# Causal 16-head attention: four banks for the maxima, two for the exponentials, one reduction for two heads

## Chip, core and metric

One core of one Trainium2 chip runs the whole program. The metric is the device time of the program in microseconds (us). The engines named below are TensorE (PE, its weight loads PEld), VectorE (DVE), ScalarE (ACT), GpSimd (POOL) and SyncE (SP, which issues DMAs). PSUM is the memory that TensorE writes its products to; it has eight banks of 512 f32 per partition.

## What is computed

The reference is eight layers on x of shape (16, 512, 128), each of the form x = x + f(layernorm(x)): causal attention with 16 heads (layer 0), a mixture of experts, window attention, the mixture again, rotary attention with 16 heads (layer 4), a channel mix, a gated delta rule, and the channel mix again. The change touches the function that builds layers 0 and 4, and by its flag `causal` only layer 0 is built differently. Layer 0 computes, per batch element:

```python
H = 16; D = C // H                       # 16 heads of 8 channels
qkv = x @ w_qkv + b_qkv                  # x: (16, 512, 128) after layernorm
scores = einsum('bhqd,bhkd->bhqk', q, k) / sqrt(D)
scores = where(tril, scores, -inf)
attn = softmax(scores)                   # over 512 keys
out = einsum('bhqk,bhkd->bhqd', attn, v)
return out @ w_out + b_out
```

## The kernel before

`attention16` works in a software pipeline over the 16 batch elements ("sequences" in the code). In the body for one index, TensorE computes the row maxima of the next element (the maxima pass) and the exponentials and their product with V for the present element (the exponential pass), besides projections, transposes and the output product of neighbours. The order of each engine's instructions is written out by hand, slot by slot.

**Slots.** A body has 32 slots `u`, in four quads of eight (`PER_QUAD`); a quad is four heads, a slot is two heads (`g` = 0 and 1) of one query tile of 128. In the causal layer a slot of the maxima pass covers W = 128 * (t + 1) keys, t = u % 8 // 2, so 128 columns in slots 0 and 1 of a quad, 256 in 2 and 3, 384 in 4 and 5, and 512 in 6 and 7 (L244). The exponential pass goes the other way: 512 columns in slots 0 and 1, 384, 256, and 128 in 6 and 7 (L245, Q0).

**TensorE's order in a slot** (L562 to L583): whatever the shared PSUM bank `misc` is used for at this slot (most even slots have one use); then for head 0 and then head 1: the scores for the maximum into `max_bank` (`max_product`, L494), the scores for the exponential into `exp_bank` (`exp_product`, L516), and two small products that add the causal mask to the former (`max_mask`, L500, the second of which tells DVE). After each odd slot of a quad follow eight products with V (`pv`, L479): after slot 1 the 128-column ones of the quad before, after slot 3 the 512-column ones (which first wait for ACT to have copied `out_bank` away, L602), after slot 5 those of 384, after slot 7 those of 256.

**Rings.** `max_bank` and `exp_bank` have three banks each (`RING`); head number h uses bank h % 3. Before a product into the maxima ring TensorE waits for the reduction of head h - 3 (`max_free`, L488); before one into the exponential ring it waits for ACT's exponential of head h - 3 (`exp_free`, L511). `out_bank` and `misc` take the other two banks.

**DVE** (L681 to L704) reduces each head's bank to one column of `M` (L687), and in some slots evacuates `misc`: in slots 14, 18, 24 and 30 it normalises four heads (L673, L676), in slot 22 it adds the output to x (L700). **ACT** (L639 to L655) does the exponential of each head (L646), in slot 2 of each quad the copy of `out_bank` (L602), and the copies out of `misc` for the transposed input (slot 0, L609), Q and K (slots 4 and 8, L617), the transposed output (slot 16, L636), V (slot 26, L624) and the maxima (slots 2, 12, 20, 28, L634). **POOL** masks the diagonal of the exponentials (L397).

A use of `misc` waits for its last evacuation, on whichever engine that is.

Of the kernel before, what the change touches and what calls it, by code (L numbers as in the profile page):

```python
# [8 lines left out]
AX = mybir.AxisListType  # L9

P = 128
B, T, C = 16, 512, 128
# [129 lines left out]
QUADS = H // 4  # L142
SLOTS = TPS * PAIRS
PER_QUAD = SLOTS // QUADS
PARTS = 3
RING = 3

Q_SLOTS = [(0, 3, 0), (3, 2, 1), (5, 1, 2)]
K_SLOTS = [(0, 3), (3, 2), (5, 1)]
# [29 lines left out]
def wait_positive(eng, sem, value):  # L179

    if not isinstance(value, int) or value > 0:
        eng.wait_ge(sem, value)


def attention16(nc, tag, io, X, stats, identity, causal, rope, biased):
    with Stage(nc, tag) as s:
# [27 lines left out]
        on = s.sb("on", [P, TPS, C])  # L214
        oT = s.sb("oT", [P, T])
        parts_dram = s.dram("parts_dram", (2, 2, PARTS, P, T), BF16)
        max_bank = s.ps("max_bank", [P, RING, T])
        exp_bank = s.ps("exp_bank", [P, RING, T])
        out_bank = s.ps("out_bank", [P, T])
        misc = s.ps("misc", [P, T])  # L220

# [36 lines left out]
        def max_head(b, u, g):  # L258

            return 2 * SLOTS * (b.off + 1) + 2 * u + g  # L260

        def exp_head(b, u, n):

            return 2 * SLOTS * b.off + 2 * u + n

        def misc_uses(b):

# [189 lines left out]
        def _(pe):  # L457
# [26 lines left out]
            def max_free(b, u, g):  # L484
                to = (b.par + 1) % 2
                if g == 0 and u % (SLOTS // 2) == 0:
                    pe.wait_ge(qk_in[to][u // (SLOTS // 2)], loads_before(b, to))
                wait_positive(pe, max_done, max_head(b, u, g) - RING + 1)  # L488

            def max_product(b, u, g):  # L490

                to = (b.par + 1) % 2
                j, t, i = u // PER_QUAD, u % PER_QUAD // 2, 2 * (u // PER_QUAD) + u % 2
                return nc.tensor.matmul(max_bank[:, max_head(b, u, g) % RING, 0:W[t]], QS[64 * g:64 * g + ROWS, to, i, t * P:(t + 1) * P],  # L494
                                        KS[64 * g:64 * g + ROWS, to, i, 0:W[t]], start=True, stop=True)

            def max_mask(b, u, g, c):

                rows, at = slice(64 * g, 64 * g + 64), (u % PER_QUAD // 2) * P + 64 * c
                return nc.tensor.matmul(max_bank[:, max_head(b, u, g) % RING, at:at + 64], mask64[rows, c, :], ident64[rows, :],  # L500
                                        start=False, stop=True, skip_group_check=True)

            def loads_before(b, to):
# [4 lines left out]
            def exp_free(b, u, n):  # L508
                if n == 0 and u % PER_QUAD == 0:
                    pe.wait_ge(shift_in[u // PER_QUAD], b.at(32, 32))  # L510
                wait_positive(pe, exp_done, exp_head(b, u, n) - RING + 1)  # L511

            def exp_product(b, u, n):
                g = EXP_ORDER[n]
                kb, i = u % PER_QUAD // 2, 2 * (u // PER_QUAD) + u % 2
                return nc.tensor.matmul(exp_bank[:, exp_head(b, u, n) % RING, Q0[kb]:T],  # L516
                                        KS[64 * g:64 * g + ROWS + 1, b.par, i, kb * P:(kb + 1) * P],
                                        QS[64 * g:64 * g + ROWS + 1, b.par, i, Q0[kb]:T],
                                        start=True, stop=True)

            def body(pe, b):
                to = (b.par + 1) % 2
                uses_at = {}
                for n, (u, what) in enumerate(misc_uses(b)):
                    uses_at.setdefault(u, []).append((what, misc_base(b) + n))

                def misc_use(what, index):
                    wait_positive(pe, misc_free, index)
                    kind = what[0]
                    if kind == "HT":  # L530
                        pe.wait_ge(hn_ready, b.at(1, 3))
                        for t in range(TPS):
                            last = nc.tensor.transpose(misc[:, t * P:(t + 1) * P], hn[:, t, :], identity[:, :])
                    elif kind in ("Q", "K", "QS", "KS"):
                        name = {"Q": "q", "K": "k", "QS": "q_swapped", "KS": "k_swapped"}[kind]
                        last = nc.tensor.matmul(misc[:, :], w[name][:, :], hT[:, b.par, :], start=True, stop=True)
                    elif kind == "V":
                        for t in range(TPS):
                            last = nc.tensor.matmul(misc[:, t * P:(t + 1) * P], hT[:, to, t * P:(t + 1) * P],
                                                    w["v"][:, :], start=True, stop=True)  # L540
                    elif kind == "MAX":
                        j = what[1]
                        seq = 0 if j == 3 else 1

                        pe.wait_ge(max_done, b.at(2 * SLOTS, (seq * QUADS + j + 1) * 2 * PER_QUAD))
                        last = nc.tensor.transpose(misc[0:H, 0:P], M[:, j % 2, :], identity[:, :])
                    elif kind == "HEADS":
                        j = what[1]
                        pe.wait_ge(heads_kept, b.at(QUADS, j + 1 - (QUADS if j == 3 else 0)))
                        for t in range(TPS):  # L550
                            last = nc.tensor.transpose(misc[:, t * P:(t + 1) * P],
                                                       heads_out[:, j % 2, t * P:(t + 1) * P], identity[:, :])
                    elif kind == "OT":
                        for t in range(TPS):
                            last = nc.tensor.transpose(misc[:, t * P:(t + 1) * P], on[:, t, :], identity[:, :])
                    else:
                        for t in range(TPS):
                            last = nc.tensor.matmul(misc[:, t * P:(t + 1) * P], oT[:, t * P:(t + 1) * P],
                                                    w["out"][:, :], start=True, stop=True)
                    last.then_inc(misc_full, 1)  # L560

                for u in range(SLOTS):  # L562
                    for what, index in uses_at.get(u, []):
                        misc_use(what, index)
                    for n in range(2):
                        if b.maxes:
                            max_free(b, u, n)
                            last = max_product(b, u, n)
                            if not causal:
                                last.then_inc(max_scores, 1)  # L570
                        if b.exp:
                            exp_free(b, u, n)
                            exp_product(b, u, n).then_inc(scores, 1)
                        if b.maxes and causal:
                            max_mask(b, u, n, 0)
                            max_mask(b, u, n, 1).then_inc(max_scores, 1)
                    for j in range(QUADS):
                        for v in range(NV):
                            slot = PER_QUAD * j + PVS[v][3]
                            if slot == u and b.exp:  # L580
                                pv(b, 0, j, v)
                            if slot == u + SLOTS and b.finish:
                                pv(b, -1, j, v)  # L583
# [4 lines left out]
        def _(act):  # L588
# [49 lines left out]
            def body(act, b):  # L638
                for u in range(SLOTS):  # L639
                    if b.exp:  # L640
                        j, n, kb = u // PER_QUAD, u % PER_QUAD, u % PER_QUAD // 2
                        wait_positive(act, pv_done, b.at(QUADS * NV, (j - 1) * NV + LAST_OF[kb]))
                        for h in range(2):
                            e = exp_head(b, u, h)
                            act.wait_ge(scores, e + 1)
                            nc.scalar.activation(probs[:, n, EXP_ORDER[h], Q0[kb]:T], exp_bank[:, e % RING, Q0[kb]:T],  # L646
                                                 ACT.Exp, scale=float(D) ** -0.5).then_inc(exp_done, 1)
                    for j in range(QUADS):
                        if u == PER_QUAD * j + KEEP_AT and b.exp:
# [10 lines left out]
        def _(dve):  # L660
# [19 lines left out]
            def body(dve, b):  # L680
                for u in range(SLOTS):  # L681
                    if b.maxes:
                        j, t = u // PER_QUAD, u % PER_QUAD // 2
                        for g in range(2):
                            col = 8 * g + 4 * (u % 2) + t
                            dve.wait_ge(max_scores, b.at(2 * SLOTS, 2 * SLOTS + 2 * u + g + 1))
                            nc.vector.reduce_max(M[:, j % 2, col:col + 1],  # L687
                                                 max_bank[:, max_head(b, u, g) % RING, 0:W[t]], AX.X)\
                                .then_inc(max_done, 1)
                    for n, (slot, what) in enumerate(misc_uses(b)):  # L690
                        if slot != u or what[0] not in ("HEADS", "Y"):
# [2402 lines left out]
```

## Time and profile before

| | us |
|---|---|
| median of 3 runs | 5264.1 |
| lowest, highest | 5263.89, 5328.75 |
| the profiled execution | 5352.55 |
| its span, first to last instruction | 5350.5 |
| causal layer within it, first product to last (62:1011) | 949 |

The profile is of one execution. Busy times are of an engine's own work and overlap between engines; a matmul's end is modelled, so a busy TensorE is not one at its peak. "PEclk" is the TensorE clock that was granted, as a share of 2.4 GHz: 1.00 is 2.4 GHz, 0.50 is 1.2 GHz, and a value between is a mean over a stretch that holds both. In a timeline row "x4" means four instructions merged into one row, and the bracket says how long the engine was idle before and what ended that.

### The profile page before, as it was taken

How to read it: one execution, taken by the hardware profiler on the slowest of the kernel's cores; microseconds unless marked ns; L12 is line 12 of the kernel's file. 1: busy time of each engine (PE TensorE's matmuls, PEld its weight loads, DVE VectorE, ACT ScalarE, POOL GpSimd, SP SyncE). 2: the span in 40 equal slices, each digit the busy share in tenths (PEclk: the TensorE clock that was granted, in tenths of full speed). 3: DMA queues.
4: the chain of work that ended last, by engine and by line, in shares of the span. 5: the costliest groups of instructions: out<-in, count | busy, mean ns of one | idle time of the engine just before them, and what ended most of it. 6: DMA issues, size and time to landing. Idle time of an engine off the chain costs nothing. (4 is left out here: it accounts for less than half of the span.)

```text
span 5350.5 us, 180273 instructions
## 1 busy us (share of the span) xinstructions
PE 4132.0 (77%) x73116; PEld 2507.2 (47%) x73118; DVE 3108.1 (58%) x7520; ACT 2378.0 (44%) x5497; POOL 1808.8 (34%) x2620
## 2 busy tenths in 40 slices
PE   4999989629359999999376399999957799996555
PEld 2443444319325555555265033333335688884223
DVE  5555555334446666665334488888676555514887
ACT  1544454305235555554043077777835433313443
POOL 3333333140455555553312422323112233302442
PEclk9776676659679999999588599999977799997777
DMA  2111111211100000000111111111001211162001
GB/s 72 46 42 40 46 40 40 64 38 52 51 11 2 3 2 2 2 2 2 50 52 52 47 45 50 49 48 49 25 2 63 84 39 45 22 194 77 24 24 33
DMA packets 252950, 218.39 MB, mean 41 GB/s; under 512 B 63683, under 2 KB 221316, under 8 KB 252550
## 3 DMA queue, kind: packets, MB, share of 16 engines
q1 hardware_dynamic: 244358, 196.20, 12.0%
q0 software_dynamic: 8192, 16.79, 1.1%
q8 instruction: 259, 4.24, 0.3%
q14 instruction: 141, 1.16, 0.1%
HBM read 139.24 MB, written 73.14 MB: 40 GB/s over the span
## 5 line engine op out<-in xcount | busy, mean ns | idle before, releaser
L687 DVE TENSOR_REDUCE l_M<-l_max_bank 128x1 f32<-128x512 f32 (+3 forms) x2048 | 1083.1, 583 | 583.6 <-PE l_max_bank L500 417.8
L646 ACT ACTIVATE l_probs<-l_exp_bank 128x512 f32<-128x512 f32 (+3 forms) x2048 | 950.0, 523 | 637.5 <-PE l_exp_bank L516 632.6
L494 PE MATMUL l_max_bank<-l_KS,l_QS 48*128 48x512 bf16 (+3 forms) x2048 | 650.5, 391 | 105.7 <-DVE l_M L687 51.2
L479 PE MATMUL l_out_bank<-l_probs,l_V 128*32 128x256 f32 (+2 forms) x6144 | 587.5, 466 | 71.3 <-ACT l_heads_out L602 71.2
L516 PE MATMUL l_exp_bank<-l_QS,l_KS 49*128 49x512 bf16 (+3 forms) x2048 | 625.3, 378 | 18.4 <-ACT l_probs L646 13.4
L397 POOL TENSOR_SCALAR_AFFINE_SELECT l_probs<-l_probs 128x256 f32<-128x256 f32 x512 | 208.0, 406 | 603.7 <-ACT l_probs L646 601.3
L494 PEld LDWEIGHTS l_max_bank<-l_KS,l_QS 48*128 48x128 bf16 x2048 | 162.0, 98 | 469.7 <-DVE l_M L687 235.8
L1841 DVE TENSOR_REDUCE l_M<-l_max_bank 128x4 f32<-128x512 f32 x256 | 175.5, 686 | 172.6 <-PE l_max_bank L1655 172.6
L479 PEld LDWEIGHTS l_out_bank<-l_probs,l_V 128*32 128x32 f32 x6144 | 137.8, 114 | 283.7 <-ACT l_probs L646 131.2
L871 POOL DMA_INDIRECT l_back<-main_sorted_out,l_index x128 | 122.5, 957 | 413.5 <-issue 413.2
L500 PE MATMUL l_max_bank<-l_ident,l_mask 64*128 64x64 bf16 x2048 | 246.1, 218 | 0.0
L1496 POOL TENSOR_TENSOR l_rms<-l_rms,l_minus_half 128x20 f32<-128x20 f32 x64 | 226.1, 3532 | 11.8 <-POOL l_rms L1493 11.8
L500 PEld LDWEIGHTS l_max_bank<-l_ident,l_mask 64*128 64x128 bf16 x2048 | 197.7, 115 | 63.9 <-issue 39.3
L436 POOL TENSOR_TENSOR l_qk<-l_qk,l_cos 128x512 f32<-128x512 f32 x32 | 40.7, 1270 | 526.6 <-ACT l_rot L620 526.4
L516 PEld LDWEIGHTS l_exp_bank<-l_QS,l_KS 49*128 49x128 bf16 x2048 | 177.9, 98 | 80.3 <-ACT l_probs L646 68.1
L969 ACT ACTIVATE l_hidden<-l_up_bank,l_own 128x128 f32<-128x128 f32 x584 | 166.4, 368 | 86.7 <-PE l_up_bank L919 86.7
L1721 ACT ACTIVATE l_raw<-l_misc 128x512 f32<-128x512 f32 (+1 forms) x192 | 101.5, 529 | 222.4 <-PE l_misc L1558 221.1
L915 PE MATMUL l_t_bank<-main_identity,l_rows 128*128 128x128 f32 x148 | 49.5, 334 | 186.0 <-DMA l_rows<-main_sorted_in 185.8
L857 POOL DMA_INDIRECT main_sorted_in<-l_hn,l_index x128 | 124.8, 975 | 189.6 <-DVE l_hn L1000 151.2
L1633 PE MATMUL l_out_bank<-l_V,l_probs 64*64 64x65 f32 x2048 | 175.8, 227 | 1.3 <-issue 1.3
L1641 PE MATMUL l_out_bank<-l_V,l_probs 64*64 64x65 f32 x2048 | 175.9, 227 | 0.0
L1635 PE MATMUL l_out_bank<-l_V,l_probs 64*64 64x65 f32 x2048 | 175.8, 227 | 0.0
(419 smaller groups left out, 10323.2 us busy)
## 6 DMA issues: line engine op xcount, KB each, us to landing
l_parts_dram<-l_parts SPq DMA_DIRECT2D x64, 384.0 KB, 2.6
l_fir_band<-in_dr_short_dram SPq DMA_DIRECT2D x16, 1024.0 KB, 6.2
l_fir_band<-in_dr_long_dram SPq DMA_DIRECT2D x16, 1024.0 KB, 8.5
l_QS<-l_parts_dram SPq DMA_DIRECT2D x128, 96.0 KB
l_KS<-l_parts_dram SPq DMA_DIRECT2D x128, 96.0 KB
l_kqv_dram<-l_in_out SPq DMA_DIRECT2D x16, 768.0 KB, 3.6
l_core_ring<-l_kqv_dram SPq DMA_DIRECT2D x48, 256.0 KB, 3.2
l_rows<-main_sorted_in SPq DMA_DIRECT2D x152, 64.0 KB, 1.8
```

The costliest lines, as they stand in the source:

```text
L397: nc.gpsimd.affine_select(out=diagonal, in_=diagonal, compare_op=ALU.is_ge, fill=0.0, base=0, pattern=[[0, 2], [1, P]], channel_multiplier ...
L479: last = nc.tensor.matmul(out_bank[STRIP * h:STRIP * (h + 1), q0:q1], V[:, par, kb, 4 * j + h, :], probs[:, 2 * kb + h // 2, h % 2, q0:q1] ...
L494: return nc.tensor.matmul(max_bank[:, max_head(b, u, g) % RING, 0:W[t]], QS[64 * g:64 * g + ROWS, to, i, t * P:(t + 1) * P], KS[64 * g:64 ...
L500: return nc.tensor.matmul(max_bank[:, max_head(b, u, g) % RING, at:at + 64], mask64[rows, c, :], ident64[rows, :], start=False, stop=True, ...
L516: return nc.tensor.matmul(exp_bank[:, exp_head(b, u, n) % RING, Q0[kb]:T], KS[64 * g:64 * g + ROWS + 1, b.par, i, kb * P:(kb + 1) * P], QS ...
L646: nc.scalar.activation(probs[:, n, EXP_ORDER[h], Q0[kb]:T], exp_bank[:, e % RING, Q0[kb]:T], ACT.Exp, scale=float(D) ** -0.5).then_inc(exp ...
L687: nc.vector.reduce_max(M[:, j % 2, col:col + 1], max_bank[:, max_head(b, u, g) % RING, 0:W[t]], AX.X)\
L1496: g.tensor_tensor(rms[:, :], rms[:, :], minus_half[:, :], ALU.pow).then_inc(rms_ready, 1)
L1633: nc.tensor.matmul(o[top], now[top, top], v, start=begin_a or (t == 0 and a == 0), stop=True, skip_group_check=True)
L1635: last = nc.tensor.matmul(o[low], now[top, low], v, start=begin_a, stop=True, skip_group_check=True)
L1641: last = nc.tensor.matmul(o[low], now[low, top], V[low, par, t, j, :], start=begin_a, stop=True, skip_group_check=True)
L1841: v.reduce_max(M[:, t % 2, h:h + REP], max_bank[:, r, :].rearrange("p (a k) -> p a k", a=REP), AX.X).then_inc(max_done, 1)
```

## The change

The three-bank rings stay for the rotary layer. In the causal layer `max_bank` gets four banks and `exp_bank` two. One reduction on DVE now reads both heads of a slot (two neighbouring banks, W columns of each) and writes two columns of `M`, eight apart. It waits until both heads' scores are masked. The semaphore `max_done` counts one per slot in place of one per head, `maxima_of` converts, and TensorE waits for it once per slot, before head 0: for the reduction of the slot two before. The exponential of head h - 2 must be done before the product of head h.

```diff
-RING = 3
+RINGS = {True: (4, 2), False: (3, 3)}
...
-        max_bank = s.ps("max_bank", [P, RING, T])
-        exp_bank = s.ps("exp_bank", [P, RING, T])
+        MAX_RING, EXP_RING = RINGS[causal]
+        max_bank = s.ps("max_bank", [P, MAX_RING, T])
+        exp_bank = s.ps("exp_bank", [P, EXP_RING, T])
...
+        def maxima_of(heads):
+
+            return (heads + 1) // 2 if causal else heads
...
-                wait_positive(pe, max_done, max_head(b, u, g) - RING + 1)
+                if g == 0 or not causal:
+                    wait_positive(pe, max_done, maxima_of(max_head(b, u, g) - MAX_RING + 1))
...
-                wait_positive(pe, exp_done, exp_head(b, u, n) - RING + 1)
+                wait_positive(pe, exp_done, exp_head(b, u, n) - EXP_RING + 1)
...
-                        pe.wait_ge(max_done, b.at(2 * SLOTS, (seq * QUADS + j + 1) * 2 * PER_QUAD))
+                        pe.wait_ge(max_done, maxima_of(b.at(2 * SLOTS, (seq * QUADS + j + 1) * 2 * PER_QUAD)))
...
-                        for g in range(2):
-                            col = 8 * g + 4 * (u % 2) + t
-                            dve.wait_ge(max_scores, b.at(2 * SLOTS, 2 * SLOTS + 2 * u + g + 1))
-                            nc.vector.reduce_max(M[:, j % 2, col:col + 1],
-                                                 max_bank[:, max_head(b, u, g) % RING, 0:W[t]], AX.X)\
+                        m, col = max_head(b, u, 0), 4 * (u % 2) + t
+                        if causal:
+                            dve.wait_ge(max_scores, m + 2)
+                            nc.vector.reduce_max(M[:, j % 2, col:col + 9:8],
+                                                 max_bank[:, m % MAX_RING:m % MAX_RING + 2, 0:W[t]], AX.X)\
+                                .then_inc(max_done, 1)
+                        for g in range(0 if causal else 2):
+                            dve.wait_ge(max_scores, m + g + 1)
+                            nc.vector.reduce_max(M[:, j % 2, col + 8 * g:col + 8 * g + 1],
+                                                 max_bank[:, (m + g) % MAX_RING, 0:W[t]], AX.X)\
                                 .then_inc(max_done, 1)
```

The other lines replace `RING` by `MAX_RING` or `EXP_RING` in the bank indices of L494, L500, L516 and L646.

## Rows read from the trace of the kernel before

**Rows 1.** The page: span, and busy time of each engine.
```profile
span 5350.5 us, 180273 instructions
PE 4132.0 (77%) x73116; PEld 2507.2 (47%) x73118; DVE 3108.1 (58%) x7520; ACT 2378.0 (44%) x5497; POOL 1808.8 (34%) x2620
```

**Rows 2.** Windows; columns: each engine's busy us, then PEclk, DMA share, GB/s.
```profile
62.00:109.00 47.00, 33.10 (x222) 18.31 (x223) 27.85 (x69) 4.19 (x8) 7.04 (x8) 1.00 0.22 71
109.00:984.00 875.00, 790.02 (x6531) 352.58 (x6526) 464.35 (x1146) 436.62 (x1184) 311.91 (x621) 0.72 0.13 40
```

**Rows 3.** Windows: the four quads of one batch element in the steady state.
```profile
564.72:581.61 16.89, 15.81 (x108) 5.67 (x105) 7.12 (x18) 7.39 (x21) 5.19 (x11) 0.60 0.15 47
581.61:597.01 15.40, 14.09 (x109) 5.87 (x104) 7.56 (x19) 7.09 (x19) 8.19 (x14) 0.60 0.15 52
597.01:611.07 14.06, 12.96 (x117) 6.55 (x112) 8.88 (x24) 6.99 (x20) 3.25 (x8) 0.71 0.18 57
611.07:622.76 11.69, 9.82 (x115) 5.44 (x113) 7.61 (x22) 6.94 (x19) 4.23 (x9) 1.00 0.02 5
```

**Rows 4.** Waits of PE, PEld in 109:984: us in total, times, longest us.
```profile
PE l_out_bank L479 <- ACT l_heads_out L602: 32.7, 61, 0.6
PE l_max_bank L494 <- DVE l_M L687: 23.0, 65, 0.5
...
PEld l_max_bank L494 <- DVE l_M L687: 85.4, 232, 1.2
PEld l_exp_bank L516 <- ACT l_probs L646: 48.3, 141, 1.4
```

**Rows 5.** DVE groups by form (first two 109:984): busy us, mean ns, idle before.
```profile
L687 DVE TENSOR_REDUCE l_M<-l_max_bank 128x1 f32<-128x512 f32 x240 | 152.6, 683 | 87.0 <-PE l_max_bank L500 87.0
...
L687 DVE TENSOR_REDUCE l_M<-l_max_bank 128x1 f32<-128x128 f32 x240 | 60.9, 286 | 64.3 <-PE l_max_bank L500 62.1
...
L1841 DVE TENSOR_REDUCE l_M<-l_max_bank 128x4 f32<-128x512 f32 x256 | 175.5, 686 | 172.6 <-PE l_max_bank L1655 172.6
```

**Rows 6.** Timeline, last slots of a quad, clock full; start, us, work, idle before.
```profile
561.82 1.29 DVE L687 TENSOR_REDUCE l_M<-l_max_bank 128x1 f32<-128x512 f32 x2 [0.84 <-PE l_max_bank L500]
563.30 0.29 DVE L676 TENSOR_TENSOR l_on<-l_misc,l_rec 128x128 f32<-128x128 f32 x1
...
562.57 0.39 PE L494 MATMUL l_max_bank<-l_KS,l_QS 48*128 48x512 bf16 x1 [0.45 <-DVE l_M L687]
563.65 0.66 PE L533 MATMUL l_misc<-main_identity,l_hn 128*128 128x128 f32 x4
```

**Rows 7.** Timeline, first four slots of a quad, clock full.
```profile
553.03 2.07 ACT L646 ACTIVATE l_probs<-l_exp_bank 128x512 f32<-128x512 f32 x4 [1.56 <-PE l_exp_bank L516]
...
556.64 0.60 ACT L602 ACTIVATE l_heads_out<-l_out_bank 128x512 f32<-128x512 f32 x1
...
553.69 0.39 PE L516 MATMUL l_exp_bank<-l_QS,l_KS 49*128 49x512 bf16 x1
...
557.39 1.06 PE L479 MATMUL l_out_bank<-l_probs,l_V 128*32 128x512 f32 x8 [0.63 <-ACT l_heads_out L602]
```

**Rows 8.** Timeline, the same slots with the clock at half.
```profile
592.85 1.29 DVE L687 TENSOR_REDUCE l_M<-l_max_bank 128x1 f32<-128x512 f32 x2 [2.44 <-PE l_max_bank L500]
...
593.60 0.61 PE L494 MATMUL l_max_bank<-l_KS,l_QS 48*128 48x512 bf16 x1
...
595.26 1.12 PE L555 MATMUL l_misc<-main_identity,l_on 128*128 128x128 f32 x4
...
597.66 0.61 PE L516 MATMUL l_exp_bank<-l_QS,l_KS 49*128 49x512 bf16 x1
...
597.01 1.08 ACT L646 ACTIVATE l_probs<-l_exp_bank 128x512 f32<-128x512 f32 x2 [2.48 <-PE l_exp_bank L516]
```

**Rows 9.** Timeline of ACT: a copy between the exponentials of slots 0 and 1.
```profile
507.67 0.61 ACT L609 ACTIVATE l_hT<-l_misc 128x512 f32<-128x512 f32 x1
508.14 1.88 ACT L646 ACTIVATE l_probs<-l_exp_bank 128x512 f32<-128x512 f32 x4
```

More of the change, by code:

```diff
@@ L493, in max_product @@
                 j, t, i = u // PER_QUAD, u % PER_QUAD // 2, 2 * (u // PER_QUAD) + u % 2
-                return nc.tensor.matmul(max_bank[:, max_head(b, u, g) % RING, 0:W[t]], QS[64 * g:64 * g + ROWS, to, i, t * P:(t + 1) * P],
+                return nc.tensor.matmul(max_bank[:, max_head(b, u, g) % MAX_RING, 0:W[t]], QS[64 * g:64 * g + ROWS, to, i, t * P:(t + 1) * P],
                                         KS[64 * g:64 * g + ROWS, to, i, 0:W[t]], start=True, stop=True)
@@ L499, in max_mask @@
                 rows, at = slice(64 * g, 64 * g + 64), (u % PER_QUAD // 2) * P + 64 * c
-                return nc.tensor.matmul(max_bank[:, max_head(b, u, g) % RING, at:at + 64], mask64[rows, c, :], ident64[rows, :],
+                return nc.tensor.matmul(max_bank[:, max_head(b, u, g) % MAX_RING, at:at + 64], mask64[rows, c, :], ident64[rows, :],
                                         start=False, stop=True, skip_group_check=True)
@@ L515, in exp_product @@
                 kb, i = u % PER_QUAD // 2, 2 * (u // PER_QUAD) + u % 2
-                return nc.tensor.matmul(exp_bank[:, exp_head(b, u, n) % RING, Q0[kb]:T],
+                return nc.tensor.matmul(exp_bank[:, exp_head(b, u, n) % EXP_RING, Q0[kb]:T],
                                         KS[64 * g:64 * g + ROWS + 1, b.par, i, kb * P:(kb + 1) * P],
@@ L645, in body @@
                             act.wait_ge(scores, e + 1)
-                            nc.scalar.activation(probs[:, n, EXP_ORDER[h], Q0[kb]:T], exp_bank[:, e % RING, Q0[kb]:T],
+                            nc.scalar.activation(probs[:, n, EXP_ORDER[h], Q0[kb]:T], exp_bank[:, e % EXP_RING, Q0[kb]:T],
                                                  ACT.Exp, scale=float(D) ** -0.5).then_inc(exp_done, 1)
```

## The prediction, made before the changed kernel had run

> **What bounds the kernel now.** The page first: a span of 5350.5 us with TensorE busy for 4132.0 of it, DVE for 3108.1 [rows 1]. Only the causal layer is built differently, so I cut the trace there. Its maxima pass runs alone for 47 us, then maxima and exponentials run together for 875 us [rows 2]: fifteen sequences of 58.04 us each (16.89 + 15.40 + 14.06 + 11.69 [rows 3], quads 0 to 3), 16% of the span. In those 875 us TensorE is busy for 790, DVE for 464, ACT for 437 [rows 2]. Neither DVE nor ACT is near full; TensorE is, but its clock is only granted at 0.72 on the mean. The quads show what that means: the one at 1.00 takes 11.69 us, those at 0.60 take 15.40 and 16.89 [rows 3]. A clock of 0.60 is a fifth of the time at full and the rest at half. So in quad 1 some 3.1 us at full do 3.1/11.69 = 0.26 of it and 12.3 us at half the remaining 0.74, or 16.7 us a quad at half. By the same step quad 0 is 19 and quad 2 16.3; quad 3 I take as 17. A sequence all at full would be 4 x 11.69 = 46.8 us, one all at half 69.
>
> Next the waits that the rings make. TensorE proper idles 23.0 us on the reductions and its weight loads 85.4 [rows 4]; the first is time in which nothing was running, the second includes time in which earlier matmuls were still at work, so a gain from the maxima ring lies between 23 and 85 us over the layer. Waits for ACT to leave a bank of the exponential ring show as 48.3 in the weight loads [rows 4]. The largest wait of TensorE proper, 32.7 us in 61 times, is none of these: it is the product with V that waits for ACT's copy of out_bank [rows 4], once in every quad.
>
> **One reduction for two.** The mean is 286 ns for 128 elements and 683 for 512 [rows 5], so 1.034 ns an element and 154 ns on top. A pair at 512 costs 154 + 1024 x 1.034 = 1.21 us, at 128 0.42. Two single ones back to back take 1.29 us from start to end [rows 6], not 1.37, because they overlap: the change takes only 0.08 us per slot off DVE, 41 us over 512 slots, on an engine that is half idle. More outputs in one reduction cost nothing: four columns out of 512 elements take 686 ns [rows 5].
>
> The Trainium skill (Perfetto Trace Analysis, Optimizing Scalar/DVE Operations) says that grouping helps where the engine is saturated, and that where it isn't but makes bubbles on others, breaking instructions up may finish work sooner. By it this step is the wrong way round; by the rows it is even, as follows.
>
> The pair starts when the second head is ready, not the first. At the end of a quad with full clock the first reduction starts at 561.82 and both are done at 563.11 [rows 6]. The second head's scores follow the first's by 0.03 us or so there (its mask product is issued right after), so the pair runs from 561.87 to 563.08: the same end. That end matters, for DVE then normalises until 563.59, and TensorE's next transposes start at 563.65 [rows 6], just behind it. **So at full clock the stall of 0.45 us before the fourth maximum product [rows 6] goes, and the wait for the normalisation takes its place: nothing gained** there.
>
> At half clock the fourth maximum product starts at 593.60, behind the first reduction as before, but the product itself takes 0.61 us, not 0.39, so TensorE comes there 0.2 later and the stall is 0.25. The transposes at 595.26 come long after DVE's first reductions are done (594.14), with a normalisation of half a microsecond behind them [rows 8]: here the 0.25 is gained. In the sequence of [rows 3] the ends of quads 0 and 1 fall at half clock, those of 2 and 3 at full: 0.25 + 0.25, and I allow 0.1 in quad 2. Gain: 0.6 us per sequence.
>
> **Two exponential banks.** In slots 0 and 1 of a quad the exponentials are 512 wide: four take 2.07 us [rows 7], so one takes 0.60 and they follow each other every 0.49. With three banks only the fourth product waits, for the first exponential: it ends at 553.63 and the product starts at 553.69 [rows 7]. With two banks the third product starts there and the fourth waits for the second exponential, which ends at 554.12: 554.18, 0.49 us later. At half clock it is the same: 597.66 is 0.05 behind the end of the first exponential of 597.01 [rows 8]; the new fourth start is 598.15. Queued behind that product are its two mask products, the products with V of the last quad, the use of misc, and slots 2 and 3. Does it reach the end? ACT itself loses nothing: the fourth product lands before ACT is through the third. Where ACT has a copy between slots 0 and 1 it is what is late: the copy at 507.67 puts the next exponentials at 508.14 and they run back to back until 510.02 into slot 2 [rows 9]. That is so in quads 0, 1 and 2 (copies of the transposed input, K, the transposed output); there I take 0.2 us, the extra latency from bank free to product to exponential, except where half clock makes TensorE the late one, in quad 2 (0.5). Quad 3 has no such copy: 0.5. Sum 0.2 + 0.2 + 0.5 + 0.5 = 1.4 us.
>
> In slots 2 and 3 the third and fourth products wait 0.4 to 0.6 us more than now, but the product with V behind them starts at 557.39, after ACT's copy (556.64 + 0.60) [rows 7], which hangs on slot 2's exponentials alone: nothing. In slots 4 and 5 the wait for the second exponential of 0.38 us lands within 0.05 of where the wait for the first reduction was: 0.2 per sequence. If the cover by ACT's copies is thinner than I think, quads 0 and 1 cost 0.5 each too: 2.0 + 0.2.
>
> **Edges.** The maxima pass alone (47 us, DVE busy 27.85 [rows 2]) saves 0.08 us in each of 32 slots, up to 2.5 us; the last sequence, with exponentials alone, loses 0.5 us in four quads: 2. Even. The DMA queue waits on the same events as before and no POOL or SP step is moved.
>
> **Sum.** 15 x (1.4 + 0.2 - 0.6) = 15 us more. Against the profiled execution, 5352.55 us with 2.05 outside its span, that is 5368; this execution is 88 us above the median, and the three runs lie between 5263.89 and 5328.75, so I carry the difference to the median: 5264.1 + 15 = **5279 us**. Bounds: all of the 85.4 us gained and nothing lost is 5179; 0.5 us lost in each of 60 quads and none gained, 5297.
>
> **The rivals.**
> *The clock falls more often.* The clock is at full for the whole of quad 3 and falls a fifth of the way into quad 0 [rows 3], just after its slots 0 and 1. The change thins TensorE's work in exactly these slots, by 0.2 to 0.5 us. If quad 3 too goes to half, it takes 17 us in place of 11.69: 5.3 us, 80 over fifteen, 5264 + 80 = 5344. If all of a sequence is at half: 15 x 11 = 165, 5429. It decides as soon as quad 3 no longer holds 1.00. For it: the clock sits at the edge, since it falls in every sequence. Against: slots 6 and 7 get denser. The Trainium skill (TensorE: Matmul & The Clock Gate, A second HAM failure mode) describes PSUM cycling whose micro-idles make the clock oscillate; quads at 0.60 and 1.00 in turn agree with it.
> *The maxima ring pays in full.* The weight loads' 85.4 us are the price, and the exponential ring's is hidden: 5264 - 85 + 5 = 5184. Against it: the transposes that sit 0.06 us behind the normalisation. With it the clock may hold: if quads 1 and 2 stay at full, 15 x (15.40 + 14.06 - 23.38) = 91 us more, 5093. It decides where TensorE stops waiting in slots 4 to 7.
> *The reduction does not join.* If DVE takes two banks in one instruction at the price of two separate starts (1.37 us), the normalisation ends 0.16 later at full clock, in two quads: 15 x 0.3 = 5 more, 5284.
>
> **Chances.** The sum as forecast, or either bound of its waits, 0.60; DVE not joining 0.05; maxima ring in full 0.12, with the clock 0.07 beside it; one more fall per sequence 0.12, all at half 0.04. A measurement of this kernel tells a change from none at about 2%, 105 us. Beyond it below lies the 0.07, above the 0.04 and part of the 0.12: slower 0.09, same 0.84. The range: 5184 and 5344 are the ends of the next cases; the runs before differ by 65 us by themselves, so I go to 5190 and 5350.
>
> **What will show it.** Right: paired reductions near 1.21 us; the weight loads' wait of L494 for DVE under 20 us; the wait of L516 for ACT over 100 us; the wait for the normalisation before L533 in its place; the full-clock quad at 12.0 to 12.2 us, and the sequence near 59. Wrong: a quad at full clock under 11.5 us, or a mean clock of the 875 us that leaves 0.72 by over 0.05 either way, which would outweigh every term above.

## The result, and the profile after

Twenty runs of the changed kernel have a median of 5279.23 us (5269.66 to 5291.3). The kernel before, run twenty times beside it, has 5326.89 (5260.22 to 5345.13). The ratio is **0.9938, 95% interval 0.9913 to 0.9964**: 0.6% faster, where I had forecast 15 us slower. The ratio is of means and leaves out the three runs of the kernel before that lie more than 1.5% above its fastest; by the medians the gain is 47.7 us. That the forecast's figure of 5279 agrees with the median is luck: it was built on 5264.1, the median of three runs of which two lay in the lower of two groups. Of the twenty runs four lie between 5260 and 5280 and sixteen between 5306 and 5345. The changed kernel has no such spread.

The page of the changed kernel, to set beside [rows 1]:

```profile
span 5281.6 us, 179763 instructions
PE 4062.9 (77%) x73118; PEld 2451.1 (46%) x73118; DVE 3078.2 (58%) x7008; ACT 2388.1 (45%) x5497; POOL 1812.4 (34%) x2620
```

The span is 68.9 us shorter; the profiled execution of the kernel before, 5352.55 us, lies above all twenty of its runs, so this is more than the 47.7 of the medians. The last exponential of the causal layer starts at 949.2 us, where it was at 1010.1, so 61 of the 68.9 are in this layer. Its windows (each engine's busy us, then PEclk, DMA share, GB/s): first the stretch with both passes, which answers to the second of [rows 2], then the four quads of one batch element (a "sequence", from the first exponential of its quad 0 to that of the next), then a quad 0, a quad 2 and a whole sequence.

```profile
103.00:938.00 835.00, 747.98 (x6625) 313.04 (x6625) 441.67 (x674) 452.15 (x1204) 317.72 (x631) 0.82 0.13 42
...
420.35:437.05 16.70, 16.13 (x104) 5.14 (x102) 6.52 (x8) 7.68 (x20) 4.95 (x10) 0.59 0.14 45
437.05:452.25 15.20, 14.30 (x108) 5.69 (x105) 6.97 (x10) 7.27 (x20) 8.22 (x14) 0.60 0.13 45
452.25:466.77 14.52, 13.19 (x117) 5.99 (x112) 8.57 (x15) 7.03 (x19) 3.35 (x8) 0.71 0.23 64
466.77:478.98 12.21, 10.39 (x115) 5.05 (x113) 7.40 (x13) 7.14 (x20) 4.50 (x9) 1.00 0.02 5
...
478.98:490.65 11.67, 10.62 (x104) 3.95 (x102) 6.48 (x8) 7.51 (x20) 4.75 (x10) 1.00 0.22 66
555.58:567.89 12.31, 10.42 (x115) 5.06 (x113) 8.57 (x16) 7.03 (x19) 3.27 (x8) 1.00 0.28 85
212.71:263.48 50.77, 44.99 (x434) 19.30 (x432) 29.29 (x46) 28.82 (x77) 20.94 (x41) 0.90 0.15 49
```

**The sequence at 420.35 has quads at 0.59, 0.60, 0.71 and 1.00, as the third to the fourteenth all had before** [rows 3], and there the two kernels can be compared at the same clock: 16.70 against 16.89, 15.20 against 15.40, 14.52 against 14.06, 12.21 against 11.69. The sum is 58.63 against 58.04: with the clock falling in the same quads, the change costs 0.6 us per sequence. But of the sequences of the changed kernel only two are like that. The others of the second to the thirteenth take 50.8 to 53.9 us, like the one at 212.71 with 0.90 of the clock and 50.77 us; ten of these twelve have a quad 0 at 1.00, before it was one. The mean clock of the stretch rises from 0.72 [rows 2] to 0.82. TensorE is busy for 747.98 us in it where it was for 790.02 [rows 2], though the change takes no product away: 42 us less of busy time in a stretch that is 40 us shorter.

The waits of PE and PEld in that stretch (us in total, times, longest us), to set beside [rows 4]:

```profile
PE l_exp_bank L522 <- ACT l_probs L652: 42.1, 110, 0.7
PE l_out_bank L484 <- ACT l_heads_out L608: 8.6, 35, 0.2
PE l_misc L557 <- DVE main_X L711: 7.8, 14, 0.6
PE l_misc L539 <- DVE l_on L682: 5.9, 13, 0.5
PE l_misc L561 <- DVE l_on L682: 4.3, 9, 0.6
PE l_max_bank L500 <- DVE l_M L693: 1.3, 2, 0.9
...
PEld l_exp_bank L522 <- ACT l_probs L652: 185.7, 460, 1.2
...
PEld l_max_bank L500 <- DVE l_M L693: 22.7, 66, 1.2
```

The kernel before, the waits of PE that [rows 4] leave out:

```profile
PE l_exp_bank L516 <- ACT l_probs L646: 8.6, 22, 0.5
PE l_misc L546 <- ACT l_hT L609: 3.4, 14, 0.4
PE l_misc L551 <- DVE main_X L700: 2.4, 14, 0.2
```

They moved as forecast. TensorE proper waited 23.0 us for the maxima ring and waits 1.3. For the exponential ring it waited 8.6 us and waits 42.1, and its weight loads 185.7 where they waited 48.3; the loads' wait for the maxima ring is 22.7, just above the "under 20" of the forecast. New in TensorE proper are the waits for DVE's normalisation before the transposes. The wait for ACT's copy of `out_bank` shrank from 32.7 us to 8.6, for part of the new wait falls ahead of it. In total TensorE proper waits 70 us in these stretches, before and after. **The 40 us come with the clock, then, not with the waits.**

Paired reductions by form (busy us, mean ns, idle before), to set beside [rows 5]: 1221 ns for twice 512 elements where 1212 was worked out, 426 for twice 128 where it was 418.

```profile
L693 DVE TENSOR_REDUCE l_M<-l_max_bank 128x2 f32<-128x1024 f32 x122 | 147.4, 1221 | 61.0 <-PE l_max_bank L506 61.0
...
L693 DVE TENSOR_REDUCE l_M<-l_max_bank 128x2 f32<-128x256 f32 x120 | 51.1, 426 | 65.3 <-PE l_max_bank L506 61.5
```

The start of a quad 3 at full clock (start, us, work, idle before), to set beside [rows 7]:

```profile
623.66 2.22 ACT L652 ACTIVATE l_probs<-l_exp_bank 128x512 f32<-128x512 f32 x4 [1.94 <-PE l_exp_bank L522]
...
624.31 0.39 PE L522 MATMUL l_exp_bank<-l_QS,l_KS 49*128 49x512 bf16 x1 [0.36 <-ACT l_probs L652]
624.80 0.39 PE L522 MATMUL l_exp_bank<-l_QS,l_KS 49*128 49x512 bf16 x1
625.12 0.43 PE L484 MATMUL l_out_bank<-l_probs,l_V 128*32 128x128 f32 x8
```

The third product starts 0.05 us after the first exponential's end and the fourth 0.49 later, at 624.80; before the change the fourth started where the third does now. The end of that quad, to set beside [rows 6]:

```profile
633.02 1.23 DVE L693 TENSOR_REDUCE l_M<-l_max_bank 128x2 f32<-128x1024 f32 x1 [0.85 <-PE l_max_bank L506]
...
634.45 0.29 DVE L682 TENSOR_TENSOR l_on<-l_misc,l_rec 128x128 f32<-128x128 f32 x1
...
634.79 0.66 PE L539 MATMUL l_misc<-main_identity,l_hn 128*128 128x128 f32 x4 [0.46 <-DVE l_on L682]
```

The stall of 0.45 us before the fourth maximum product is gone, and in its place TensorE waits 0.46 us for the normalisation (634.45 + 0.29), before the transposes. The end of a quad 0 has no normalisation. The kernel before had the same stall there at full clock, and the changed kernel has no wait of TensorE at that place:

```profile
172.59 0.39 PE L494 MATMUL l_max_bank<-l_KS,l_QS 48*128 48x512 bf16 x1 [0.45 <-DVE l_M L687]
```

### The profile page after: what moved, and what is told of

Same layout as the page of the kernel before. It is cut to its first block and busy times, and to the rows that moved or that the text cites. A ratio compares the mean times of both kernels' runs of the same rounds, so it can differ in the third digit from the quotient of the medians.

```text
span 5281.6 us, 179763 instructions
## 1 busy us (share of the span) xinstructions
PE 4062.9 (77%) x73118; PEld 2451.1 (46%) x73118; DVE 3078.2 (58%) x7008; ACT 2388.1 (45%) x5497; POOL 1812.4 (34%) x2620
## 5 line engine op out<-in xcount | busy, mean ns | idle before, releaser
L698 DVE TENSOR_REDUCE l_M<-l_max_bank 128x1 f32<-128x512 f32 x1024 | 635.2, 681 | 157.6 <-PE l_max_bank L500 157.3
L500 PE MATMUL l_max_bank<-l_KS,l_QS 48*128 48x512 bf16 (+3 forms) x2048 | 620.6, 376 | 80.6 <-DMA l_KS<-l_parts_dram 45.2
L693 DVE TENSOR_REDUCE l_M<-l_max_bank 128x2 f32<-128x256 f32 (+3 forms) x512 | 416.1, 824 | 386.7 <-PE l_max_bank L506 382.0
L484 PE MATMUL l_out_bank<-l_probs,l_V 128*32 128x256 f32 (+2 forms) x6144 | 558.0, 444 | 48.2 <-ACT l_heads_out L608 45.8
L500 PEld LDWEIGHTS l_max_bank<-l_KS,l_QS 48*128 48x128 bf16 x2048 | 159.8, 97 | 393.4 <-DVE l_M L698 147.1
L1507 POOL TENSOR_TENSOR l_rms<-l_rms,l_minus_half 128x20 f32<-128x20 f32 x64 | 226.2, 3534 | 11.8 <-POOL l_rms L1504 11.6
L506 PE MATMUL l_max_bank<-l_ident,l_mask 64*128 64x64 bf16 x2048 | 229.2, 208 | 0.0
```

The source lines that it names most:

```text
L484: last = nc.tensor.matmul(out_bank[STRIP * h:STRIP * (h + 1), q0:q1], V[:, par, kb, 4 * j + h, :], probs[:, 2 * kb + h // 2, h % 2, q0:q1] ...
L500: return nc.tensor.matmul(max_bank[:, max_head(b, u, g) % MAX_RING, 0:W[t]], QS[64 * g:64 * g + ROWS, to, i, t * P:(t + 1) * P], KS[64 * g ...
L506: return nc.tensor.matmul(max_bank[:, max_head(b, u, g) % MAX_RING, at:at + 64], mask64[rows, c, :], ident64[rows, :], start=False, stop=T ...
L693: nc.vector.reduce_max(M[:, j % 2, col:col + 9:8], max_bank[:, m % MAX_RING:m % MAX_RING + 2, 0:W[t]], AX.X)\
L698: nc.vector.reduce_max(M[:, j % 2, col + 8 * g:col + 8 * g + 1], max_bank[:, (m + g) % MAX_RING, 0:W[t]], AX.X)\
L1507: g.tensor_tensor(rms[:, :], rms[:, :], minus_half[:, :], ALU.pow).then_inc(rms_ready, 1)
```

## The experiments

Two theories were set against each other. **Ring theory:** the change wins because TensorE waits less, by four banks or by the joined reduction. **Clock theory:** at equal clock the change loses a little; it wins since the kernel before falls into step with the granted clock, the same falls in each sequence, and any change to the length of a sequence breaks that step. In e2 to e8 layers 1 to 7 are left out (`build(nc, io, layers=(0,))`), so that only the causal layer counts; their times are compared with each other. e2 to e4 ran on one chip and e5 to e8 on another; the whole kernel before, run beside them, has medians of 5325.16 and 5336.91 us, 0.2% apart, where the differences that are read across the two groups are 2.7% and more.

**e1: the kernel before, unchanged.**

> The unchanged kernel once more, for a second trace of it and for the spread of its time. Clock theory: its 20 earlier runs lie in two groups, four from 5260 to 5280 us and sixteen from 5306 to 5345; a trace of the lower group must show the causal layer's sequences shorter than 58 us at a mean clock above 0.72 and the quads at clock 1.00 still at 11.7 us; one of the upper group must repeat the 58.04 us. Ring theory (the change wins by its waits): the groups have nothing to do with the causal layer, its sequences are 58 us in either.

Measured: 5330.99 us (5261.21 to 5339.96, 12 runs), ratio 0.9991 (0.9965 to 1.0017). One run of twelve, 5261.21 us, is in the lower group; its mean clock over the program is 0.857, that of the others 0.838 to 0.847. The traced one (5320.52 us) has the same 58.0 us from its fourth sequence to the thirteenth; the first row is such a sequence, the second a quad 0 of an early sequence that had the full clock:

```profile
320.96:378.96 58.00, 52.64 (x434) 23.54 (x432) 31.16 (x79) 28.42 (x77) 20.84 (x42) 0.71 0.13 43
155.32:167.21 11.89, 10.03 (x107) 4.26 (x105) 7.07 (x18) 7.28 (x20) 5.19 (x11) 1.00 0.21 67
```

So the step is no accident of one execution. No run of the lower group has a trace, so what its sequences look like is not shown.

**e2: layer 0 of the kernel before, alone.**

> The kernel before with layers 1 to 7 left out (load, layer norm, causal attention, store), for a time in which only the causal layer counts. From the trace of before: load and norm 62 us, layer 949, store some 10 to 20: 1025 to 1040 us if the clock falls twice per sequence as in that trace; 960 to 990 in runs where it does not. Clock theory: both values occur, or a value between them. Ring theory: one value near 1030.

Measured: 1018.14 us (1006.96 to 1027.11). Three of the six runs lie at 1006.96 to 1011.68 and three at 1024.60 to 1027.11: two values, as clock theory had it, but neither of them near its 960 to 990, and the upper near the 1030 of ring theory. The times alone don't decide. The trace (1006.96 us, clock 0.778) says more: six sequences of 46 to 58 us first, then the step sets in with the seventh, and each takes 57.98 to 58.03 us from there to the thirteenth. The second row is one of those; the first is a quad 2 of the free part.

```profile
284.38:296.48 12.10, 9.94 (x115) 5.45 (x113) 8.87 (x25) 6.94 (x20) 3.25 (x8) 1.00 0.29 85
593.00:651.03 58.03, 52.67 (x435) 23.53 (x432) 31.18 (x79) 28.43 (x77) 20.86 (x42) 0.71 0.13 42
```

Over its six runs the time goes with the mean clock: 1006.96 us at 0.778, 1027.11 at 0.751.

**e3: layer 0 of the changed kernel, alone.**

> The changed kernel, layer 0 alone in the same way. Its trace had the layer in some 890 us, so 965 to 985 us. Both theories agree on that value; clock theory adds that it comes with a mean clock near 0.80 in the layer and that a quad at clock 1.00 between slots 24 and 31 takes 12.2 us (11.7 before), ring theory that quads at equal clock are shorter than before.

Measured: 970.11 us (968.1 to 973.13). By the medians the lone layer is 48 us faster than e2 and the whole program 47.7, so the gain is in this layer. Quad 3 at full clock takes 12.21 us in this trace, as clock theory had it and ring theory not (11.69 [rows 3]). This kernel falls into a step of its own, two sequences of 52.16 and 50.24 us in turn, with more of the clock:

```profile
474.45:526.61 52.16, 46.53 (x434) 19.62 (x432) 29.30 (x46) 28.83 (x77) 20.93 (x41) 0.87 0.14 48
526.61:576.85 50.24, 43.88 (x434) 18.93 (x432) 29.44 (x46) 28.83 (x78) 20.93 (x41) 0.93 0.15 48
```

**e4: the rings of 4 and 2, one reduction per head.**

> Layer 0 alone; four banks for the maxima and two for the exponentials, but one reduction per head as before the change. My steps: joining the reductions is even, so at equal clock the quads equal those of the changed kernel within 0.1 us. Clock theory: the time goes by where the clock falls, 960 to 1040 us, and the quads at 1.00 take 12.0 to 12.2. Ring theory: within 5 us of the changed kernel's layer. If the joined reduction is what wins: near the kernel before.

```diff
-                        if causal:
+                        if False:                      # one reduction per head, as before
...
-                        for g in range(0 if causal else 2):
+                        for g in range(2):
-                if g == 0 or not causal:
+                if True:
-            return (heads + 1) // 2 if causal else heads
+            return heads
```

Measured: 971.94 us (960.31 to 986.31), the same as e3 within its runs, as both theories allowed. Quads 0, 2 and 3 at full clock, and a quad 1 at 0.60:

```profile
201.78:213.46 11.68, 10.42 (x104) 3.78 (x101) 7.22 (x18) 7.51 (x21) 4.75 (x10) 1.00 0.22 67
331.42:343.70 12.28, 10.25 (x116) 5.00 (x113) 8.88 (x25) 7.06 (x19) 3.27 (x8) 1.00 0.25 88
343.70:355.88 12.18, 10.22 (x116) 4.99 (x113) 7.91 (x22) 7.13 (x20) 4.50 (x9) 1.00 0.05 14
213.46:228.65 15.19, 14.29 (x108) 5.70 (x105) 7.66 (x19) 7.26 (x20) 8.41 (x15) 0.60 0.13 46
```

11.68, 12.28, 12.18 and 15.19 against 11.67, 12.31, 12.21 and 15.20 of the changed kernel: joining two reductions gives nothing; it takes 0.03 us in quads 2 and 3. The reduction alone isn't what wins.

**e5: rings of 3 and 2. One bank less, nothing in return.**

> Layer 0 alone; the only edit to the kernel before is that the exponential ring has two banks (maxima keep three, one reduction per head). By the steps: at clock 1.00 the last quad goes from 11.70 to 12.2 us, as in the changed kernel, since it is the exponential ring that costs there. Ring theory (a change that only takes a bank away can only lose): slower than 1018 us by 10 to 30. Clock theory: the sequence no longer comes to 58.03 us, the falls of the clock spread out, and the time is 960 to 990 us although nothing was given in return for the bank.

```diff
-RINGS = {True: (4, 2), False: (3, 3)}                  # on top of e4
+RINGS = {True: (3, 2), False: (3, 3)}
```

Measured: **978.32 us (966.47 to 1011.55), 40 us faster than e2**, though this kernel only lost a bank. Four of its six runs lie at 966.47 to 980.67; the other two, 1004.48 and 1011.55, are as long as the shorter three of e2. Ring theory, which had it 10 to 30 us slower, falls here. Quads 0, 2 and 3 at full clock, the sequence that holds them, the one sequence in the old pattern, and a quad 1 and a quad 2 at a lower clock:

```profile
216.04:228.07 12.03, 10.76 (x104) 4.03 (x102) 7.20 (x18) 7.63 (x20) 5.20 (x11) 1.00 0.22 65
240.78:253.07 12.29, 10.61 (x115) 5.23 (x113) 8.88 (x25) 7.14 (x19) 3.27 (x8) 1.00 0.27 87
253.07:265.26 12.19, 10.57 (x115) 5.22 (x113) 7.91 (x22) 7.25 (x19) 4.25 (x9) 1.00 0.04 15
...
216.04:265.26 49.22, 43.33 (x434) 18.86 (x432) 31.57 (x79) 29.29 (x77) 20.94 (x42) 0.97 0.16 50
156.70:216.04 59.34, 54.95 (x434) 22.31 (x432) 31.77 (x79) 29.29 (x77) 20.93 (x42) 0.71 0.13 41
...
433.17:448.72 15.55, 14.50 (x108) 5.67 (x105) 7.66 (x19) 7.26 (x19) 8.22 (x14) 0.61 0.15 51
448.72:463.26 14.54, 13.41 (x117) 6.13 (x112) 8.99 (x24) 7.14 (x19) 3.26 (x8) 0.71 0.17 56
```

In the old pattern a sequence is 59.34 us against 58.03, so at equal clock the missing bank does cost 1.3 us. What it gains by is that the pattern doesn't repeat: the next sequence is 49.22 us at 0.97.

**e6 and e7: more work for TensorE, rings of three.**

> Layer 0 alone, kernel before, rings of three; in slots 0 and 1 of quad 0 each exponential product is issued twice (the same product into the same bank), which adds four 512-column products per sequence, 0.2 us each at full clock and 0.4 at half: 10 to 20 us more work over the layer. Ring theory: 1025 to 1040 us. Clock theory: the fall at slot 2 of quad 0 needs TensorE's thin work just there and the repeat after 58.03 us; with either gone, 970 to 1000 us, faster with more work.

> The same four doubled products per sequence, but in slots 24 and 25 (start of quad 3, where the clock is at full in the kernel before). If it is the work just before the fall (slots 0 and 1 of quad 0) that decides: the clock still falls there in every sequence, 1025 to 1035 us. If it is the length of a sequence as a whole that keeps the pattern: it is broken here too, 970 to 1000 us.

```diff
                             exp_free(b, u, n)
+                            if causal and u in (0, 1):          # e7: (24, 25)
+                                exp_product(b, u, n)            # the same product once more
                             exp_product(b, u, n).then_inc(scores, 1)
```

Measured: 956.94 us (932.85 to 975.59) for e6 and 951.88 (945.16 to 962.64) for e7, **61 and 66 us faster than e2 with 64 more products of 512 columns in each**. In e6 alone the cause could be that TensorE is busier just before the fall in quad 0. But e7 leaves quad 0 as it was and touches quad 3, and it does the same. A quad 3 of e7 and the quad 0 behind it at full clock:

```profile
606.27:618.18 11.91, 10.14 (x117) 5.34 (x114) 7.66 (x21) 6.95 (x19) 4.24 (x9) 1.00 0.03 11
618.18:630.07 11.89, 10.03 (x107) 4.26 (x105) 7.07 (x18) 7.29 (x20) 5.21 (x11) 1.00 0.20 65
```

Quad 3 is 0.2 us longer than before (11.91 for 11.69). Quad 2 is longer by as much, for it ends with the first exponential of quad 3, which comes later; so a sequence is 0.4 us longer. Quad 0 is what it was (11.89), and it now has the clock. So the fall can go with nothing changed in the work just before it, in slots 0 and 1 of quad 0. That it is the length is not shown by e7 alone: it also gives TensorE more work in quad 3, ahead of the place of the fall.

**e8: the changed kernel with the products with V moved.**

> Layer 0 alone, changed kernel; the products with V that stood after slot 1 of each quad go after slot 0, where TensorE would wait for the two-bank exponential ring, and those that stood after slot 3 (behind ACT's copy of out_bank) go after slot 4. By the steps this takes up to 0.5 us of the exponential ring's wait and up to 0.6 us of the wait for the copy off each quad: at clock 1.00 quads of 11.2 to 11.8 us in place of 11.7 to 12.3, and 15 to 50 us off the layer's 970 at the same clock, 920 to 955. If those waits are hidden anyway: 965 to 975.

```diff
-            PVS = [(0, 0, T, 3), (1, P, T, 5), (2, 2 * P, T, 7), (3, 3 * P, T, 9)]
+            PVS = [(0, 0, T, 4), (1, P, T, 5), (2, 2 * P, T, 7), (3, 3 * P, T, 8)]
```

Measured: 943.87 us (931.15 to 945.12), 26 us faster than e3, inside the first expectation for the time. At full clock quads 2 and 3 take 11.89 and 12.10 us for 12.31 and 12.21, so quad 2 gained 0.4 us and quad 3 only 0.1, and neither is within the 11.2 to 11.8 expected. This kernel is in step too, one sequence like the other:

```profile
510.32:561.53 51.21, 46.25 (x438) 19.66 (x440) 29.47 (x46) 29.19 (x78) 20.93 (x41) 0.87 0.16 48
```

In step it takes 51.2 us a sequence, and so does e3 as the mean of its two: there the shorter quads are paid for by a lower clock, 0.87 against 0.90. In the traces e8 is ahead by the sequences before and after the steady part.

**e9: the whole program with e7's doubled products.**

> The whole program, kernel before with the four doubled products in slots 24 and 25 of the causal layer and nothing else. Alone the layer went from 1018 to 952 us. Clock theory: the whole goes from 5325 to about 5260, faster with more work. If the other layers give it back or the lone layer misleads: 5325 or above.

Measured: 5263.93 us median, ratio to the kernel before **0.9869 (0.9835 to 0.9903)**. This is of five runs at 5256.31 to 5274.46; a sixth took 5641.89 us at a mean clock of 0.691. A kernel that only does more work than the one before beats it by 1.3%. One of its sequences has the clock's old pattern (quads at 0.60, 0.60, 0.71 and 1.00), and it is 0.4 us longer than 58.03; the next takes 48.67 us:

```profile
410.45:468.92 58.47, 53.21 (x438) 23.64 (x436) 31.28 (x79) 28.44 (x77) 20.90 (x42) 0.71 0.13 42
```

**e10: the whole program with rings of 3 and 2.**

> The whole program, kernel before with only the exponential ring of the causal layer cut to two banks. Alone the layer went from 1018 to 978 us. Clock theory: 5285 to 5290, so that most of what the change brings comes with its costly half alone. Ring theory: 5335 to 5350.

Measured: 5291.58 us (5279.48 to 5318.61), ratio 0.9919 (0.9892 to 0.9947). Clock theory had 5285 to 5290, ring theory 5335 to 5350. Its interval overlaps that of the change.

**e11 and e12: the whole program with the products with V moved, rings before and after.**

> The whole program; rings of three and one reduction per head as before, but the products with V moved from slots 3 and 9 to 4 and 8. From the quads at clock 1.00: without the two-bank ring's 0.1 to 0.5 us per quad it should be 10 to 20 us better than the changed kernel with the same move if the clock is granted alike, so 5235 to 5250; if its sequences fall into step with the clock again as before, 5290 to 5320.

> The whole program; the changed kernel with the products with V moved. Alone the layer went from 970 to 944 us, so 5279 - 26 = 5253, faster than both kernels. If it is hidden in the whole: 5275 to 5285.

Measured: e12 5254.35 us (5252.06 to 5258.37), ratio 0.9851 (0.9822 to 0.988). **e11, with three banks in each ring and a reduction for each head, 5199.21 us (5197.78 to 5201.55), ratio 0.9747 (0.9719 to 0.9776)**: faster than the kernel before, the changed one and everything else here, and better than I expected. With this move the change loses 55 us (e12). The shortest kind of sequence of e11 and its quad 3, then the longest kind; and from e12 a quad 2, a quad 3 and a sequence:

```profile
346.39:392.84 46.45, 39.69 (x438) 18.95 (x440) 31.56 (x79) 28.02 (x78) 20.91 (x42) 0.96 0.16 52
381.55:392.84 11.29, 9.52 (x119) 5.28 (x121) 7.71 (x22) 6.96 (x20) 4.24 (x9) 1.00 0.07 20
440.79:489.60 48.81, 42.39 (x438) 19.57 (x440) 31.50 (x79) 28.07 (x78) 20.91 (x42) 0.90 0.15 50
```

```profile
592.81:604.69 11.88, 10.47 (x119) 5.08 (x120) 8.54 (x16) 7.03 (x19) 3.26 (x8) 1.00 0.29 89
604.69:616.79 12.10, 10.38 (x119) 5.12 (x120) 7.42 (x13) 7.20 (x19) 4.50 (x9) 1.00 0.05 15
360.76:411.98 51.22, 46.22 (x438) 19.70 (x439) 29.46 (x45) 29.12 (x77) 20.91 (x41) 0.87 0.14 47
```

At full clock the move takes 0.5, 0.6 and 0.4 us off quads 0, 2 and 3 of the kernel before (11.37, 11.47 and 11.29 for 11.89, 12.10 and 11.69) and, by quads at 0.75, some 0.3 off quad 1 (13.42 for 13.72 in e2). That is 1.8 us a sequence or 27 over fifteen, as an estimate; the kernel gained 128 by the medians. The rest goes with the clock, which e11 has at 0.93 over its steady part. e11 is in step with it too, but over four sequences: 47.93, 46.44, 47.96 and 48.81 us, and the same again. e12 is in step at 51.22 us and 0.87. Of the 55 us between them some 18 are no matter of the clock: at full clock quads 2 and 3 take 11.88 and 12.10 us in e12 for 11.47 and 11.29, 1.2 us a sequence. What of the rest is the clock's is not separated.

## Why the prediction was wrong

**The step that failed is the last one of the sum, "15 x (1.4 + 0.2 - 0.6) = 15 us more".** It multiplies a cost per sequence by fifteen and so takes the granted clock as it was. The cost per sequence was nearly right (0.6 measured at the same clock pattern, 1.0 forecast); what was left out is that the edit itself changes where the clock falls. In the traces the sequences go from 58.04 us to 50.8 to 53.9 in most cases, 4 to 7 us a sequence, a term larger than all the others and of the other sign. The prediction had named the sign of this under "Wrong": a mean clock that leaves 0.72 by over 0.05. It is 0.82.

The steps before it, against the rows:

- *One reduction for two*: even, as forecast. 1221 ns for 1212; e4 against the changed kernel, at most 0.03 us a quad.
- *The end of a quad at full clock*: right to the hundredth for quad 3. The stall of 0.45 went and 0.46 us behind the normalisation came. But "nothing gained" at full clock holds only where a normalisation stands behind the maxima. At the end of quad 0 none does, and the stall of 0.45 (the row at 172.59) goes at full clock too.
- *Two exponential banks*: forecast 0.2, 0.2, 0.5 and 0.5 us in quads 0 to 3. e5 against the kernel before at like clock: 12.03 for 11.89, 15.55 for 15.40 at 0.60, 12.29 for 12.10 at full (14.54 for 14.06 at 0.71), 12.19 for 11.69. So 0.14, 0.15, 0.2 to 0.5, 0.5, with the 0.05 for slots 4 and 5 inside.
- *Four banks for the maxima*: forecast 0.25 in quads 0 and 1, 0.1 in 2, nothing in 3. e4 against e5: 0.35 (11.68 for 12.03, at full clock) and 0.36 (15.19 for 15.55), then 0.01 and 0.01. Over a sequence in the old pattern the two terms measure 1.3 (59.34 for 58.03, e5) and 0.7 (58.63 for 59.34) where I had 1.6 and 0.6: together the 0.6 for the 1.0.
- *The rivals.* The clock was named as one, with the wrong sign: I took a thinner start of quad 0 to mean more falls. The twelve quads 0 between the second and the thirteenth sequence of the changed kernel have the thinner start, and ten keep the clock. A case "the clock falls less often with nothing else gained" was in none of my chances; I had tied a better clock to the maxima ring paying in full.
- *The base.* Three runs of a kernel with two groups of times gave a median of 5264, the profiled one 5352. The prediction saw a gap of 88 us, wrote it down and carried on from the median. That gap is larger than any term of the sum; it was the sign that something of that size can switch.

What the experiments show and what they don't: that the gain is the clock's is shown (the busy time and the waits of the two traces; and e5, e6, e7, e9 and e10 gain without a bank or a joined reduction given, three of them with more work). That the old kernel's step hangs on the sequence's length is argued. For it: the old pattern of the clock comes up in the changed kernel (58.63 us), in e5 (59.34) and in e9 (58.47), but it repeats only where it takes 58.03. Against calling it shown: every one of these edits also moves TensorE's work or waits about, and none lengthens a sequence and nothing else. It was also not tried to bring the step back, by shortening the changed kernel's sequence by 0.6 us. Nor do the edits end the locking: e3, e8, e11 and e12 are each in a step of their own, at 0.90, 0.87, 0.93 and 0.87 of the clock. Which step a kernel falls into, and why the clock falls at slot 2 of quad 0 in one sequence and not in the next, with the same instructions, is open.

## What to carry to other kernels

Where a loop's period repeats to the hundredth of a microsecond while the granted clock is between its levels, and runs of one kernel form two groups, compare stretches at equal clock first: they say what an edit costs, while the total may say mostly where the clock fell. Don't keep an edit for its total alone; here a bank given away and 64 useless products "gained" as much as the change. And look for the largest wait of the bound engine itself: moving the products with V, two numbers in one list, took it away (32.7 us for ACT's copy of `out_bank`). The kernel was 2.5% faster; about 0.5% is this move at equal clock, an estimate from the quads of e11, and the rest went with the clock.

## What was not expected of the hardware

- The granted clock and a periodic kernel lock: 58.03 us in sequence after sequence in two executions of the kernel before and in its lone layer (e2), 51.21 in e8 and e12, 52.16 and 50.24 in turn in e3, four sequences that come again in e11. TensorE is busy for 52.67 of 58.03 us in such a sequence (e2) while its clock is at 0.71.
- The lock takes hold during the run (after six sequences in e2, after three in e1) and then holds to the end of the stretch with both passes.
- More TensorE work can go with a shorter time: e9, 64 products more, 1.3% less.
- In step, shorter quads need not shorten the sequence: e3 and e8 both take 51.2 us, at 0.90 and 0.87 of the clock.
- Two reductions back to back in 1.29 us against one of 1.22 over both: a reduction more costs 0.07 us when DVE has the next at hand, half of the 0.15 that its duration shows.
